# Step 0's normalisation, turn and query projection placed among the parts of batch 3 of the first layer, with value buffers exchanged and loads in batch 3

## The chip, the cores and the metric

The kernel runs on one core of one Trainium2 chip. The metric is the device time of one execution in microseconds (us), lower is better; "the time before" is the median of three executions.

The five engines run their own instruction lists in order and meet only through semaphores: TensorE (PE in the profile, with its weight loads as PEld), VectorE (DVE), ScalarE (ACT), GpSimd (POOL) and SyncE (SP), which here only issues DMAs. An instruction whose semaphore has not arrived holds up all that stands behind it in its engine's list.

## The reference

Four stages are added to a residual stream `x` of 4 batches, 512 tokens, width 128, each on the layer norm of the stream before it.

```python
x = x + _L0_xcond_ref(ctx, ln(x), cond, cond, ...)   # 16 heads of 64: queries from x, keys and values from ctx rows 512 + 77
x = x + _L0_ffn_ref(ln(x), ...)                       # ternary weights, activations rounded to 127 levels, relu squared
x = x + _L1_xcond_ref(ln(x), cond, ctx, masks, ...)   # 6 layers
x = x + _L1_ffn_ref(ln(x), ...)                       # 8 experts, each token goes to one

for i in range(6):                                    # inside _L1_xcond_ref, 16 heads of 8
    xn = _adaln(x, noise_emb, n1_w[i], n1_b[i])       # gain and bias of the norm come from emb @ w.T + b
    q, k, v = split(xn @ qkv_w[i].T); q, k = _rope(q), _rope(k)
    x = x + _attn(q, k, v, src_mask) @ so_w[i].T      # softmax over 512 keys
    xn = _adaln(x, ..., n2)                           # cross attention to 77 context rows, then
    x = x + _attn(_rope(xn @ cq_w.T), _rope(ctx @ ck_w.T), ctx @ cv_w.T, ctx_mask) @ co_w[i].T
    x = x + gelu(_adaln(x, ..., n3) @ f1_w[i].T + f1_b[i]) @ f2_w[i].T + f2_b[i]
```

## The kernel before

**Stages.** The first attention layer with its feed-forward part ("the first layer" here) is worked off batch by batch, `bt` = 0 to 3. For one batch there are 32 pairs of (head pair `u`, 128 queries `q`): `scores` (PE), `maximum` (DVE), `exp` (ACT), `divide` (DVE makes 1/sum, POOL multiplies), `turn` (PE transposes), `turned` (DVE and ACT copy), and 40 parts `weigh` (PE, weights times values), then four parts `out` (PE, L1402), the output projection. After the last `out` of batch 3, its feed-forward part `b_stats`, `b_norm`, `b_square`, `b_power`, `b_scale`, `b_quant`, `b_turn`, `b_up`, ... is still to come; it runs among the parts of the next stage.

The six later layers are 24 steps `m` = 4*layer + batch. A step's self attention is: `s_stats` (DVE) and `s_norm` (POOL, L2361 to L2367), `s_turn` (PE) and `s_mod` (ACT), the projections `qk` 0 and 1 (PE, L1614), the rotation `qk_rope` 0 to 3 (DVE, L2033), a swap of rows by four DMAs each for q and k (`q_swap`, `k_swap`, L1153), `q_thirds` and `k_thirds` (POOL, L2373 to L2383, a split of each float into three bf16 parts), six DMAs each that write the parts into the stacks `q_st` and `k_st` (`q_rows` L1197, `k_rows` L1208), then 64 parts `maximum` (PE L1467, DVE L1977), `shift` (POOL), `shift_turn` and `shift_out` (PE, ACT), one DMA `shift_rows` for each half (L1211), and 64 parts `scores` (PE L1455), `exp` (ACT L2197) and 16 `weigh` (PE L1487).

**Fixed rows.** Some rows of the stacks hold zeros, ones and the mask. `first_zeros` and `first_rows` write those of step 0. `other_rows` (18 DMAs of SP, L1104 to L1148) writes those of all other batches and of the cross attention; every `maximum` of a step above 0 waits for it (`zeroed`), and its DMAs stand in SP's one list like all the others.

**Gains.** `condition(i)` (PE, L1276) multiplies the norm weights `nT` with the condition vector in five pieces; ACT copies (L2111) and POOL adds the bias (L2325) as `gains`.

**What sets the order.** A table per engine gives each part a place and so an order in steady state. `PLACED_TENSOR`, `PLACED_SCALAR`, `PLACED_VECTOR`, `PLACED_POOL`, `PLACED_SYNC` override it around the seam between the stages: an entry `("maximum", 11, 0): [("b_turn", 0, None)]` says that `b_turn` 0 of the last batch runs just before `maximum` 11 of step 0. A PSUM bank is waited for by who writes it next (`free(b)`): `BANKS["qk"] = [0, 6]`, `BANKS0["out"] = [6]`, and `BANKS0["weigh"]` ends with bank 6.

**Value buffers.** The first layer's values lie in two buffers in turn. One of them is the space `wl` of the later layers' weights:

```python
handle.tensor_copy(v0[bt % 2][i][0:rows, 0:512], ...)   # batches 1 and 3 in wl
```

so that layer 0's weights of the next stage can be loaded only when batch 3's `weigh` is done (`av`).

Of the kernel before, what the change touches and what calls it, by code (L numbers as in the profile page):

```python
# [40 lines left out]
MAGIC = 1.5 * 2.0 ** 23  # L41
NORM_PIECES = ((0, 2), (2, 6), (6, 16), (16, 26), (26, 36))
# [54 lines left out]
def build(nc, a, out):  # L97

    ctx = ExitStack()
    with ctx:  # L100
# [5 lines left out]
        def bank(i):  # L106
            return psum[:, i, :]
# [55 lines left out]
        nT = A0[:, A_NT:A_NT + 6 * NL * D]  # L163
        early = (taken[0] - 4 * S - A_NT) // D
# [31 lines left out]
        lat_set, ctx_set, ffn_set = norm_set(), norm_set(), norm_set()  # L196
# [45 lines left out]
        st_s, mv_s, ve_s, rs_s = step_norm()  # L242
# [41 lines left out]
        DONE_ROWS = STEPS - B + 3  # L284

# [11 lines left out]
        def four(t):  # L297
# [219 lines left out]
            ("scores", 1, 0): [("maximum", 38, 0)],
            ("maximum", 40, 0): [("maximum", 39, 0)],
            ("maximum", 41, 0): [("scores", 2, 0)],
            ("scores", 3, 0): [("maximum", 42, 0)],  # L520
            ("weigh", 0, 0): [("scores", 7, 0), ("s_turn", 0, 1)],
            ("scores", 9, 0): [("maximum", 45, 0)],
            ("scores", 10, 0): [("maximum", 46, 0)],
            ("maximum", 47, 0): [("qk", 0, 1)],
            ("scores", 12, 0): [("maximum", 48, 0), ("scores", 11, 0)],
            ("scores", 13, 0): [("qk", 1, 1)],
            ("scores", 15, 0): [("weigh", 1, 0)],
            ("scores", 17, 0): [("scores", 16, 0)],
            ("scores", 19, 0): [("maximum", 50, 0)],
            ("maximum", 52, 0): [("maximum", 51, 0), ("weigh", 2, 0), ("v", 0, 1)],  # L530
# [18 lines left out]
            ("maximum", 17, 1): [("scores", 42, 0)],
            ("maximum", 20, 1): [("maximum", 19, 1), ("scores", 45, 0)],  # L550
            ("scores", 48, 0): [("maximum", 22, 1)],
            ("maximum", 24, 1): [("scores", 51, 0)],
            ("maximum", 26, 1): [("weigh", 11, 0)],
# [1989 lines left out]
```

## Time and profile before

| | |
|---|---|
| time before | 2364.84 us median (2360.6, 2364.84, 2368.64) |
| the profiled execution | 2367.46 us, of which its span (first to last instruction) 2365.3 us |
| busy share of the span | PE 94%, PEld 41%, DVE 82%, ACT 74%, POOL 46% |
| mean granted TensorE clock | 0.975 of full speed |
| busy tenths of PE in 40 slices of 59 us | 6999999999688999999999999999999999999979 |
| granted clock in the same slices | 9999999999589999999999999999999999999979 |
| the chain that ended last | PE 63%, DVE 14%, ACT 10%, DMA 4%, POOL 4%, issue 3% |

How to read it: each digit is a tenth of a slice, and a granted clock of 5 is the lower of TensorE's two levels. The slices 11 to 13 (591 to 768 us) are the seam between the first layer and step 0 to 2 of the next stage.

### The profile page before, as it was taken

The numbers are of one execution on the slowest core, as the hardware profiler recorded it, in microseconds if no ns is written. First come the engines' busy times: TensorE is split into PE (matmuls) and PEld (weight loads), VectorE is DVE, ScalarE is ACT, GpSimd is POOL, SyncE is SP. The second block draws the span as 40 slices with busy tenths as digits, with TensorE's granted clock in tenths as the row PEclk, the third lists the DMA queues.
The fourth block names the chain that finished last, engine by engine and source line by source line (L and its number), as shares of the span: only waits on it lengthen the run. The fifth ranks groups of instructions, "written<-read, shape, count | busy, mean of one in ns | idle before, by whom it ended". The sixth has DMA issues, their size and how long they took to land.

```text
span 2365.3 us, 46233 instructions
## 1 busy us (share of the span) xinstructions
PE 2218.9 (94%) x17034; PEld 960.1 (41%) x17034; DVE 1930.4 (82%) x3983; ACT 1761.9 (74%) x3601; POOL 1082.6 (46%) x1348
## 2 busy tenths in 40 slices
PE   6999999999688999999999999999999999999979
PEld 3455455545322333333343333333343334333336
DVE  6778889698778888888888888898888888888435
ACT  4778778696166778788888787887888887777744
POOL 3656556466334434434444443533454444432324
PEclk9999999999589999999999999999999999999979
DMA  2000000000312211212222321212222322111000
GB/s 84 2 1 1 1 2 1 30 1 20 90 50 63 82 50 54 65 46 72 62 67 69 82 63 48 67 51 66 54 74 63 81 63 66 49 49 52 25 23 19
DMA packets 108570, 113.07 MB, mean 48 GB/s; under 512 B 15809, under 2 KB 96951, under 8 KB 107319
## 3 DMA queue, kind: packets, MB, share of 16 engines
q1 hardware_dynamic: 108345, 110.12, 17.1%
q8 instruction: 135, 2.21, 0.4%
q14 instruction: 90, 0.74, 0.1%
HBM read 14.80 MB, written 1.05 MB: 7 GB/s over the span
## 4 chain that ended last, share of the span: by engine, by line
PE 63%; DVE 14%; ACT 10%; DMA 4%; POOL 4%; issue 3%; SPq 2%; DVEq 0%; POOLq 0%; ACTq 0%
PE psum L1487 11%; PE psum L1455 6%; PE psum L1467 6%; DVE A L1977 5%; PE psum L1258 4%; PE psum L1599 4%; PE psum L1591 4%; PE psum L1559 3%; PE psum L1388 3%; PE psum L1342 3%; DMA A<-A 3%; ACT A L2137 3%; DVE A L1999 3%; PE psum L1548 2%; PE psum L1354 2%
## 5 line engine op out<-in xcount | busy, mean ns | idle before, releaser
L1977 DVE TENSOR_REDUCE A<-psum 128x1 f32<-128x512 f32 x1536 | 969.9, 682 | 141.5 <-PE psum L1467 133.4
L2197 ACT ACTIVATE A<-psum 128x512 f32<-128x512 f32 x1536 | 821.4, 604 | 206.0 <-PE psum L1455 177.9
L1467 PE MATMUL psum<-A 64*128 64x512 bf16 x1536 | 421.8, 391 | 35.9 <-DVE A L1977 12.8
L1455 PE MATMUL psum<-A 64*128 64x512 bf16 x1536 | 403.9, 384 | 15.6 <-DVE A L1977 6.0
L1487 PE MATMUL psum<-A 128*9 128x512 f32 (+1 forms) x3072 | 405.2, 604 | 1.6 <-ACT A L2197 1.5
L2342 POOL TENSOR_TENSOR A<-A,rden 128x512 f32<-128x512 f32 x256 | 266.7, 1067 | 177.5 <-DVE rden L1862 176.7
L2373 POOL TENSOR_TENSOR A<-A 128x512 f32<-128x512 f32 (+1 forms) x78 | 96.6, 1239 | 301.8 <-DMA A<-A 291.8
L1467 PEld LDWEIGHTS psum<-A 64*128 64x128 bf16 x1536 | 105.1, 94 | 309.7 <-DVE A L1977 116.7
L2227 ACT ACTIVATE A<-psum 77x512 f32<-77x512 f32 x384 | 199.7, 598 | 30.3 <-PE psum L1548 29.7
L1455 PEld LDWEIGHTS psum<-A 64*128 64x128 bf16 x1536 | 103.5, 94 | 277.2 <-DVE A L1977 103.8
L2137 ACT ACTIVATE A<-psum,nm 128x512 f32<-128x512 f32 x256 | 176.0, 688 | 45.0 <-DVE nm L1850 44.1
L2386 POOL CAST A<-A 128x32 bf16<-128x32 f32 (+1 forms) x72 | 15.7, 218 | 384.3 <-DVE A L1999 197.9
L1999 DVE TENSOR_REDUCE A<-psum 128x8 f32<-128x616 f32 x192 | 149.9, 793 | 22.0 <-PE psum L1531 18.5
L1258 PE MATMUL psum<-ident,A 128*128 128x128 f32 x880 | 141.5, 288 | 21.0 <-DVE A L1724 14.5
L1846 DVE TENSOR_REDUCE mins<-psum 128x2 f32<-128x1024 f32 x128 | 155.2, 1212 | 5.4 <-PE psum L1342 5.2
L1342 PE MATMUL psum<-A 64*128 64x512 f32 x512 | 142.0, 617 | 1.8 <-DVE mins L1834 1.8
L1258 PEld LDWEIGHTS psum<-ident,A 128*128 128x128 f32 x880 | 96.1, 143 | 95.8 <-issue 55.4
L2361 POOL TENSOR_SCALAR A<-A 128x4 f32<-128x4 f32 x72 | 16.3, 227 | 213.0 <-DVE A L1967 213.0
L1548 PE MATMUL psum<-A 64*77 64x512 bf16 x384 | 104.6, 410 | 4.1 <-DMA A<-A 2.1
L1559 PE MATMUL psum<-A 77*32 77x512 f32 (+1 forms) x768 | 105.6, 623 | 1.7 <-ACT A L2227 1.6
L1354 PEld LDWEIGHTS psum<-ident,A 64*128 64x128 f32 x2048 | 76.0, 139 | 73.0 <-issue 48.9
L1591 PE MATMUL psum<-A,wl 128*128 128x512 f32 x192 | 97.0, 628 | 1.0 <-ACT A L2197 0.5
(209 smaller groups left out, 3743.4 us busy)
## 6 DMA issues: line engine op xcount, KB each, us to landing
A<-A SPq DMA_DIRECT2D x456, 128.0 KB, 2.4
A<-A SPq DMA_DIRECT2D x336, 64.0 KB, 2.0
A<-zero SPq DMA_DIRECT2D x51, 128.0 KB, 2.4
wl<-in_wl SPq DMA_DIRECT2D x6, 1024.0 KB, 5.8
A<-A SPq DMA_DIRECT2D x36, 78.0 KB, 2.1
A<-in_nT SPq DMA_DIRECT2D x1, 1664.0 KB, 6.8
A<-in_w SPq DMA_DIRECT2D x2, 512.0 KB, 7.0
A<-in_w SPq DMA_DIRECT2D x1, 1024.0 KB, 6.1
```

The costliest lines, as they stand in the source:

```text
L1258: t = handle.transpose(psum[:, b, q * P:(q + 1) * P], src[:, q, :], ident[:, :])
L1342: handle.matmul(bank(b), q_pair[lo:lo + HD0, u % 2, q * P:(q + 1) * P], k_pair[lo:lo + HD0, u % 2, 0:S], start=True, stop=True).then_inc(s ...
L1455: handle.matmul(bank(b), k_st[bt][lo:lo + ROW, h // 2, k * P:(k + 1) * P], q_st[m % 3][lo:lo + ROW, h // 2, :], start=True, stop=True).the ...
L1467: handle.matmul(bank(b), q_st[m % 3][lo:lo + ROW, pair, q * P:(q + 1) * P], k_st[bt][lo:lo + ROW, pair, :], start=True, stop=True).then_in ...
L1487: t = handle.matmul(psum[32 * j:32 * j + (HW if g % 2 else 32), b, :], values, pT[:, i % 2, j, :], start=k == 0, stop=k == QT - 1)
L1591: handle.matmul(bank(b), wcols(m, W_F1 + i * P, P), xnT_f, start=True, stop=True).then_inc(f1_ps, 1)
L1977: handle.tensor_reduce(nm[:, pair // 4, q, j, pair % 4:pair % 4 + 1], bank(BANKS["maximum"][i]), AX.X, ALU.max, negate=True).then_inc(mx, 1)
L1999: handle.tensor_reduce(cnm[:, :, :, i], both, AX.X, ALU.max, negate=True).then_inc(cm, 1)
L2137: handle.activation(p0[r][:, j, :], bank(BANKS0["scores"][i][j]), ACT.Exp, bias=nm0[:, r, j:j + 1], accum_out=c_p[:, n, j, q, C:CP]).then_ ...
L2197: handle.activation(pT[:, block % 2, i % GROUP, :], bank(BANKS["scores"][i]), ACT.Exp, scale=HD1 ** -0.5).then_inc(ex, 1)
L2227: handle.activation(cpT[0:C, g % 2, i % GROUP, :], psum[0:C, BANKS["cross_scores"][i], :], ACT.Exp, scale=HD1 ** -0.5).then_inc(cex, 1)
L2342: handle.tensor_tensor(p0[i % 4][:, j, :], p0[i % 4][:, j, :], rden[:, u % 2, j, q:q + 1].to_broadcast([P, S]), ALU.mult).then_inc(dp, 1)
```

## The change

All of it is at that seam.

1. Value buffers are exchanged: `v0[(bt + 1) % 2]`, so batches 0 and 2 use `wl` and batches 1 and 3 the other buffer.
2. Loads: when batch 2 is done, layer 0's weights go to `wl[:, 0]` and the first 16 pieces of `nT` to `wl[:, 1]`. The other 20 pieces and the small cross mask are loaded at the end of batch 3 (`late_loads`). The mask comes as 8 rows of 512 instead of 2 rows of 2048.
3. Step 0's `s_stats`, `s_norm`, `s_turn`, `s_mod`, `qk` 0 and `qk_rope` 0 and 1, `condition` and `gains` 0 and `fixed_rows` 0 run among the parts of batch 3. `qk` 1 stands between the last `weigh` and `out`.
4. The fixed rows of step 0 are written by separate parts `zero_q`, `rows_q`, `zero_k`, `rows_k`; `other_rows` is placed just before `q_swap` of step 1.
5. The orders of steps 0 to 4 are other tables.

```diff
-        v0[bt % 2]
+        v0[(bt + 1) % 2]
...
         PLACED_TENSOR = {
-            ("qk", 0, 0): [("condition", 0, None)],
-            ("v", 0, 0): [("condition", 1, None), ("condition", 2, None)],
-            ("maximum", 0, 0): [("condition", 3, None)],
-            ("maximum", 11, 0): [("b_turn", 0, None)],
+            ("turn", 16, -1): [("condition", 0, -1)],
+            ("weigh", 20, -1): [("s_turn", 0, 0)],
+            ("weigh", 31, -1): [("qk", 0, 0)],
+            ("out", 0, -1): [("qk", 1, 0)],
+            ("v", 0, 0): [("condition", 1, -1), ("condition", 2, -1)],
+            ("maximum", 0, 0): [("condition", 3, -1), ("condition", 4, -1)],
+            ("maximum", 16, 0): [("b_turn", 0, -1)],
...
         PLACED_VECTOR = {
+            ("divide", 14, -1): [("s_stats", 0, 0)],
+            ("divide", 26, -1): [("fixed_rows", 0, -1)],
+            ("divide", 30, -1): [("qk_rope", 0, 0)],
+            ("turned", 29, -1): [("qk_rope", 1, 0)],
...
         PLACED_POOL = {
+            ("divide", 39, -1): [("gains", 0, -1)],
+            ("divide", 40, -1): [("s_norm", 0, 0)],
+            ("shift", 0, 0): [("gains", 1, -1), ("b_power", 0, -1), ("gains", 2, -1), ("constants", 0, -1), ("b_power", 1, -1)],
...
         PLACED_SYNC = {
-            ("q_swap", 0, 0): [("first_rows", 0, 0)],
-            ("k_swap", 0, 0): [("q_zero", 0, 0)],
-            ("shift_rows", 0, 0): [("other_rows", 0, 0)],
+            ("q_swap", 0, 0): [("masks", 0, 0), ("weights", 0, 0), ("zero_q", 0, 0)],
+            ("k_swap", 0, 0): [("late_loads", 0, 0), ("rows_q", 0, 0)],
+            ("k_rows", 0, 0): [("zero_k", 0, 0), ("q_zero", 0, 0), ("rows_k", 0, 0)],
+            ("shift_rows", 0, 0): [("q_rows", 0, 0)],
+            ("q_swap", 0, 1): [("other_rows", 0, 0)],
...
+                if name == "late_loads":
+                    sp.wait_ge(av, B * NP0)
+                    sp.wait_ge(in_mask, 16)
+                    sp.wait_ge(in_late, 112)
+                    handle.dma_start(maskc_i[0:2, :], a["maskc"]).then_inc(in_mask, 16)
+                    handle.dma_start(norm_w(NORMS_FIRST, 6 * NL), a["nT"][:, NORMS_FIRST * D:]).then_inc(in_late, 16)
+                if name == "other_rows":
+                    sp.wait_ge(prep_ps, 1 + len(NORM_PIECES))
+                    sp.wait_ge(ow, B)
+                    sp.wait_ge(fixed, 3)
```

In the placements, the third number -1 stands for batch 3 of the first layer.

The order on TensorE at the end of batch 3, in the kernel before (L1388 is `weigh`, L1276 `condition`, L1402 `out`, L1258 `s_turn`, L1614 `qk`, L1622 `v`, L1467 `maximum`):

```order
L1388 MATMUL psum<-A 64x512 [waits tc_a]
L1388 MATMUL psum<-A 64x512
L1276 MATMUL psum<-condT,A 128x4 x2
L1402 MATMUL psum<-A 128x128 [waits av_a]
L1402 MATMUL psum<-A 128x128 x31
L1258 MATMUL psum<-ident,A 128x128 [waits s_y]
L1258 MATMUL psum<-ident,A 128x128 x3
L1276 MATMUL psum<-condT,A 128x4 [waits in_late]
L1276 MATMUL psum<-condT,A 128x4 x3
L1614 MATMUL psum<-A,wl 128x512 [waits in_wl,s_xn]
L1614 MATMUL psum<-A,wl 128x512 [waits x0]
```

The same place in the changed kernel, whose lines are 25 to 27 higher (L1411 is `weigh`, L1641 `qk` 1, L1423 `out`, L1301 `condition`, L1649 `v`, L1494 `maximum`):

```order
L1411 MATMUL psum<-A 64x512 [waits tc_a]
L1411 MATMUL psum<-A 64x512
L1641 MATMUL psum<-A,wl 128x512 [waits av_a]
L1423 MATMUL psum<-A 128x128 [waits qk_ro]
L1423 MATMUL psum<-A 128x128 x31
L1301 MATMUL psum<-condT,wl 128x4 x14
L1649 MATMUL psum<-wl,A 128x128 x4
L1301 MATMUL psum<-condT,A 128x4 [waits in_late]
L1301 MATMUL psum<-condT,A 128x4 x9
L1301 MATMUL psum<-condT,A 128x4 [waits g_copied]
L1301 MATMUL psum<-condT,A 128x4 x9
L1494 MATMUL psum<-A 128x512 [waits rows,k_rows,q_rows]
```

`qk` 1 has come ahead of `out`, and since both use bank 6, `out` now waits until DVE has read `qk` 1 (`qk_ro`); `s_turn` and `qk` 0 have gone up into batch 3.

SP's list between the rows of step 0 and the swaps of step 1, before (L1208 is `k_rows` of step 0, L1104 to L1148 `other_rows`, L1211 `shift_rows` 0 of step 0, L1153 `q_swap` of step 1):

```order
L1208 DMA A<-A 16x8x512 [waits sp_k]
L1104 DMA A<-zero 16x24x512 [waits prep_ps]
L1104 DMA A<-zero 16x24x512
L1104 DMA A<-zero 16x16x512
L1104 DMA A<-zero 16x32x284
L1104 DMA A<-zero 16x16x312
L1108 DMA A<-A 2x16x512 [waits zeroed]
...
L1148 DMA A<-A 2x16x312
L1211 DMA A<-A 16x4x512 [waits sh_T]
L1153 DMA A<-A 32x512 [waits qk_ro]
```

The same in the changed kernel (L1233 is `q_rows` of step 0, L1248 `shift_rows`, L1115 to L1181 `other_rows`, L1186 `q_swap` of step 1):

```order
L1233 DMA A<-A 16x8x512 [waits sp_q]
L1248 DMA A<-A 16x4x512 [waits sh_T]
L1115 DMA A<-zero 16x24x512 [waits fixed,ow,prep_ps]
L1115 DMA A<-zero 16x24x512
L1115 DMA A<-zero 16x16x512
L1115 DMA A<-zero 16x32x284
L1115 DMA A<-zero 16x16x312
L1119 DMA A<-A 2x16x512 [waits zeroed]
...
L1181 DMA A<-A 2x16x312
L1186 DMA A<-A 32x512 [waits qk_ro]
```

`shift_rows` 0 has moved ahead of the 18 DMAs of `other_rows`, which now stand between it and the swaps of step 1.

POOL's list from the split of step 0's q to its first shift, before (L2373 to L2383 are `q_thirds`, then `k_thirds`; L2311 is `b_power`; L2315 to L2317 `constants`; L2361 the start of `s_norm` of step 1):

```order
L2311 TENSOR_TENSOR A<-A,neg_half 128x4 [waits b_ve]
...
L2373 TENSOR_TENSOR A<-A 128x512 [waits q_swap,qk_ro]
...
L2311 TENSOR_TENSOR A<-A,neg_half 128x4 [waits b_ve]
L2373 TENSOR_TENSOR A<-A 128x512 [waits k_swap,qk_ro]
...
L2315 MEMSET A 128x256 [waits ow]
L2316 MEMSET A 128x1344
L2317 MEMSET A 128x2016
L2361 TENSOR_SCALAR A<-A 128x4 [waits s_mv,s_yT]
```

The same in the changed kernel (L2394 to L2404 are the splits, L2332 is `b_power`, L2336 to L2338 `constants`, L2407 `shift`):

```order
L2394 TENSOR_TENSOR A<-A 128x512 [waits q_swap,qk_ro]
...
L2394 TENSOR_TENSOR A<-A 128x512 [waits k_swap,qk_ro]
...
L2332 TENSOR_TENSOR A<-A,neg_half 128x4 [waits b_ve]
...
L2336 MEMSET A 128x256 [waits ow]
L2337 MEMSET A 128x1344
L2338 MEMSET A 128x2016
L2332 TENSOR_TENSOR A<-A,neg_half 128x4 [waits b_ve]
L2407 CAST A<-A 128x8x4 [waits mx]
```

Both `b_power` now stand behind both splits, and `constants` has come in between the two of them.

## Rows read from the trace of the kernel before

**Rows 1.** Windows: length, busy PE, PEld, DVE, ACT, POOL, clock, DMA share, GB/s

```profile
540.00:580.00 40.00, 39.36 (x375) 19.58 (x372) 32.23 (x66) 32.75 (x94) 28.61 (x28) 1.00 0.01 2
...
680.00:694.00 14.00, 10.96 (x52) 4.45 (x52) 9.19 (x15) 6.28 (x10) 3.62 (x6) 0.63 0.06 17
```

**Rows 2.** Timeline, end of batch 3: start, length, engine; in brackets its wait

```profile
584.47 1.03 PE L1388 MATMUL psum<-A 77*64 77x512 f32 x4
585.55 0.60 ACT L2158 ACTIVATE A<-psum 128x512 f32<-128x512 f32 x1 [2.89 <-PE psum L1388]
586.20 7.41 PE L1402 MATMUL psum<-A 128*128 128x128 f32 x64 [0.16 <-ACT A L2158]
593.65 0.69 DVE L1874 TENSOR_TENSOR x_res<-x_res,psum 128x512 f32<-128x512 f32 x1 [1.83 <-PE psum L1402]
```

**Rows 3.** Timeline, step 0's q and k up to its first maximum

```profile
598.84 0.69 DVE L2033 TENSOR_TENSOR A<-psum,sinT 128x512 f32<-128x512 f32 x1 [2.98 <-PE psum L1614]
603.99 1.27 POOL L2373 TENSOR_TENSOR A<-A 128x512 f32<-128x512 f32 x1 [0.24 <-DMA A<-A]
612.03 4.04 SPq L1208 DMA_DIRECT2D A<-A  x6
617.94 1.03 PE L1467 MATMUL psum<-A 64*128 64x512 bf16 x4 [6.24 <-issue]
```

**Rows 4.** Timeline, feed-forward part of batch 3 up to DVE's first maximum

```profile
602.57 0.86 DVE L1706 BATCH_NORM_STATS2 A<-A 128x6 f32<-128x128 f32 x4
605.31 0.17 DVE L1736 TENSOR_SCALAR A<-A 128x4 f32<-128x4 f32 x1
609.05 1.04 POOL L2311 TENSOR_TENSOR A<-A,neg_half 128x4 f32<-128x4 f32 x1
610.12 1.28 ACT L2162 ACTIVATE A<-A 128x128 f32<-128x128 f32 x4 [7.06 <-POOL A L2311]
611.43 1.12 DVE L1886 TENSOR_TENSOR A<-A 128x512 f32<-128x512 f32 x1 [5.95 <-ACT A L2162]
614.42 4.69 DVE L1945 TENSOR_SCALAR A<-A,small 128x128 f32<-128x128 f32 x4
621.15 18.22 DVE L1977 TENSOR_REDUCE A<-psum 128x1 f32<-128x512 f32 x30
```

**Rows 5.** One line of DVE, all 32 instances: shortest, median, longest in ns

```profile
L1945 DVE TENSOR_SCALAR A<-A,small x32: 269/479/4241, 204.9 to 678.5; 128x128 f32<-128x128 f32 x16, 128x512 f32<-128x512 f32 x16
```

**Rows 6.** Timeline, POOL's divides late in batch 3

```profile
542.31 4.18 POOL L2342 TENSOR_TENSOR A<-A,rden 128x512 f32<-128x512 f32 x4 [4.04 <-DVE rden L1862]
...
572.91 6.16 POOL L2342 TENSOR_TENSOR A<-A,rden 128x512 f32<-128x512 f32 x6 [2.13 <-DVE rden L1862]
```

**Rows 7.** Timeline of SP's DMA issues, then what SP waited for, 615 to 665

```profile
616.12 7.88 SPq L1104 DMA_DIRECT2D A<-zero  x5
...
630.13 5.95 SPq L1120 DMA_DIRECT2D A<-A  x3
...
638.31 1.32 SPq L1148 DMA_DIRECT2D A<-A  x1
645.84 0.61 SPq L1211 DMA_DIRECT2D A<-A  x1
660.06 2.50 SPq L1153 DMA_DIRECT2D A<-A  x4
...
SPq L1153 <- DVE A L2033: 14.2, 1, 14.2
...
SPq L1108 <- DMA A<-zero: 3.9, 1, 3.9
```

**Rows 8.** Timeline, step 1's q and k up to its first maximum

```profile
656.69 1.10 PE L1614 MATMUL psum<-A,wl 128*128 128x512 f32 x2 [0.35 <-ACT A L2197]
...
665.96 1.26 POOL L2373 TENSOR_TENSOR A<-A 128x512 f32<-128x512 f32 x1
...
678.83 0.60 PE L1467 MATMUL psum<-A 64*128 64x512 bf16 x3
```

More of the change, by code:

```diff
@@ L516, in build @@
+            ("maximum", 29, 0): [("b_up", 3, -1)],
             ("maximum", 37, 0): [("maximum", 36, 0)],
[L517 to L518 removed]
+            ("maximum", 38, 0): [("scores", 0, 0)],
             ("maximum", 41, 0): [("scores", 2, 0)],
             ("scores", 3, 0): [("maximum", 42, 0)],
[L521 removed]
+            ("scores", 6, 0): [("maximum", 43, 0), ("maximum", 44, 0)],
@@ L522, in build @@
+            ("scores", 8, 0): [("s_turn", 0, 1)],
             ("scores", 9, 0): [("maximum", 45, 0)],
[L523 to L530, printed above, removed]
+            ("maximum", 47, 0): [("qk", 0, 1), ("maximum", 46, 0)],
@@ L548, in build @@
             ("weigh", 8, 0): [("maximum", 15, 1)],
[L549 to L553, printed above, removed]
+            ("weigh", 9, 0): [("maximum", 17, 1)],
+            ("o_turn", 0, 0): [("maximum", 18, 1)],
+            ("maximum", 20, 1): [("maximum", 19, 1)],
@@ L850, in build @@
         PLACED_VECTOR = {
-            ("qk_rope", 0, 0): [("fixed_rows", 0, None), ("x_out", 0, None), ("b_stats", 0, None)],
-            ("qk_rope", 2, 0): [("b_norm", 0, None)],
-            ("max", 0, 0): [("b_square", 0, None), ("b_quant", 0, None), ("s_stats", 0, 1)],
-            ("max", 30, 0): [("b_affine", 0, None)],
-            ("max", 33, 0): [("b_stats2", 0, None)],
-            ("max", 35, 0): [("b_stats2", 1, None)],
-            ("max", 36, 0): [("b_stats2", 2, None)],
-            ("max", 40, 0): [("b_stats2", 3, None)],
@@ new lines, in build @@
+            ("divide", 26, -1): [("fixed_rows", 0, -1)],
+            ("divide", 30, -1): [("qk_rope", 0, 0)],
+            ("turned", 29, -1): [("qk_rope", 1, 0)],
+            ("max", 0, 0): [("x_out", 0, -1), ("b_stats", 0, -1), ("b_norm", 0, -1), ("b_square", 0, -1), ("s_stats", 0, 1),
+                ("fixed_rows", 1, -1), ("b_quant", 0, -1)],
+            ("max", 30, 0): [("b_affine", 0, -1)],
+            ("max", 31, 0): [("b_stats2", 0, -1)],
+            ("max", 35, 0): [("b_stats2", 1, -1)],
@@ L1189, in part @@
                         sp.wait_ge(sh_rows, 32 * (m - 2))
+                    if m == 0:
+                        for done in (pq, pk, pc):
+                            sp.wait_ge(done, NP0 * B)
+                    else:
+                        sp.wait_ge(ow, B)
+                        sp.wait_ge(fixed, 2)
                     sp.wait_ge(q_rows, 112 * m)
@@ L1449, in part @@
                 l, bt = divmod(m, B)
+                if name == "warm":
+                    b = EXPERTS_BANKS["warm"][m // (STEPS - 1)][i]
+                    free(b)
+                    for _ in range(4):
+                        handle.matmul(bank(b), zero16[:, 0:P], zero16[:, :], start=True, stop=True)
+                    owner.pop(b, None)
                 if name == "scores":
```

490 lines of the change are left out of this document (247 added, 243 removed).

## The prediction

> **What bounds the kernel now.** I read the page's slices first: TensorE is busy nine tenths nearly everywhere except at both ends and in the three slices from 591 to 768 us, where its granted clock falls too. So a change at this seam can only be worth what the seam wastes. The windows come next: late in batch 3 PE is busy 39.4 of 40 us, so work put there is not free on PE, while POOL has 11 idle us in the same stretch [rows 1]. The timeline then gives two chains that run side by side from the last `weigh` to the first maximum of step 0.
>
> Chain one is step 0's q and k. The last `weigh` ends at 585.5, `out` runs from 586.2 to 593.6 [rows 2]; only then come `s_turn` and `qk`, the rotation at 598.84, the split on POOL at 603.99, the last six row DMAs at 612.03, and PE's first maximum at 617.94, after 6 us in which it did nothing [rows 3]. Chain two is the feed-forward part of batch 3: `x_out` at 593.65 [rows 2], `b_square` ready at 605.5, but `b_power` 1 only at 609.05, as it stood behind the split of q; `b_scale` at 610.12; `b_quant` from 611.43; DVE's first maximum at 621.15 [rows 4]. Chain two ends later, by 2.6 us of maxima that already lay ready. It decides.
>
> Behind both comes a third list that no engine waits for yet: SP's. `other_rows` took it from 616.12 to 639.6, 23.5 us, with 3.9 us of waiting for its own zeros. After that SP waited for DVE 14.2 us, until 660.06 when step 1's first rotation was done [rows 7]. The reader is to see that this slack of SP is as large as all that the change can win.
>
> **The change part by part.**
>
> *Batch 3 gets longer.* PE takes up `condition` 0, `s_turn` and `qk` 0. A projection like `qk` takes 1.1 us where it stands at step 1 [rows 8]; the other two are smaller. Bounds 0 (all inside PE's waits) and 3.3; I take 2.1, near the top, because PE is full. `condition` 0 stood between `weigh` and `out`, so there it gives back what it costs here, which I count below. POOL's `s_norm` and `gains` 0 are some 4 us and are put exactly where POOL waited 4.04 us for DVE; before POOL becomes the one waited for, at 572.91, it still has waits, the last of 2.13 [rows 6]. Cost nothing; without that cover 4. DVE's additions (`s_stats`, two rotations at 0.69 [rows 3], `fixed_rows` 0) are some 4 us in a stretch where DVE is idle 7.8 of 40 us [rows 1]; I count them within the 2.1.
>
> *`out` waits.* Before, `out` began when ACT had copied the last `weigh` [rows 2]. Now `qk` 1 needs that same copy (bank 6), and `out` needs bank 6 back from DVE: 1.0 for `qk` 1 and 1.3 for two rotations, 2.3 us. `out` ends at 593.6 + 2.1 + 2.3 = 598.0.
>
> *Chain one* now runs beside `out`: ACT's copy is done at 588.2, k's rotation starts at 589.2, its split on POOL 5.15 later as before (603.99 - 598.84 [rows 3]), at 594.4, and it ends near 599.9. SP then has k's six row DMAs and behind them q's six, 4.0 each; with the fixed rows ahead of them they start near 598 and the first maximum could run at 598 + 8.1 + 1.9 = 608.
>
> *Chain two* decides again. From the end of `out`: `x_out` and `b_stats` 2.2, `b_power` 0 1.0 after 0.3 of waiting for POOL's split of k, `b_norm` 1.4, `b_square` 2.9 (602.57 to 605.48 [rows 4]; POOL's `constants` fall into it and are over before it), `b_power` 1 1.0, `b_scale` 1.3. `b_quant` and what follows took 8.5 us until `s_stats` of step 1 began, of which 4.69 for four small operations [rows 4]; one of them took 4.24 where the shortest of the line takes 0.27 [rows 5], and POOL was filling memory then. That filling now lies earlier, and `s_stats` 1 is ahead of `b_quant`: 4.5. With four hand-overs of 0.2 this is 15.4, so DVE's first maximum comes at 613.4 instead of 621.15, **7.7 us earlier**.
>
> *What is late next.* Step 0's maxima and `b_up` keep their distances, so `shift_rows` 0, 24.7 us behind the first maximum before (645.84 [rows 7]), is issued at 613.4 + 24.7 + 0.5 (one more statistics operation ahead of the 32nd maximum) = 638.6; 0.6 later SP starts `other_rows`. It has stood idle for some 30 us by then, but its list had the shift first. 639.2 + 23.5 = 662.7: only now do the swaps of step 1 go out, though DVE has had the rotation since 660.06 - 7.7 = 652.4. Before they went out at 660.06. Then POOL: four swaps take 2.5, landing 1.6, so its split starts at 666.8; before it started at 665.96, held by work of its own [rows 8]. PE's first maximum of step 1 came 12.9 us later, at 678.83 [rows 8]; now at 679.7. Behind it in PE's list stand the rest of step 0's scores and `weigh`, the second shift's transposes and `b_turn2`, so ACT and DVE run dry too, DVE after its 64 maxima, near 671. PE stands some 8 us. **The 7.7 us are given back, and 0.9 more.**
>
> One correction: of the three mask DMAs (5.95 us, L1120 [rows 7]) none should need more than the 0.7 that the DMAs beside them take, so up to 3.9 may not come again. I take half of it, 1.9.
>
> The Trainium skill weighs the other way: "DMA: Bandwidth & Descriptors", section "Issuing engines are not separate DMA queues", says that the sequencer's time to start a DMA is usually small beside the DMA itself. By that rule the 18 DMAs would cost next to nothing in SP's list and the kernel would win all of the 7.7 us, 2357; the issue rows, 23.5 us for the block, say otherwise for this kernel.
>
> **The sum.** +0.9 - 1.9 = -1.0 us: the profiled execution's span of 2365.3 becomes 2364.3, its time of 2367.5 becomes 2366.5. That execution lies 2.6 above the median of the runs, so the median becomes 2363.8. What remains of the pipeline is the same work in nearly the same order; I give it nothing.
>
> **The rivals.**
>
> *The gain comes through* (faster). If `other_rows` holds SP for less than 13 us (639.2 to 652.4), the swaps of step 1 follow DVE and all 7.7 us stay: 2357, and up to 9.8 with batch 3's additions hidden: 2355. For it: 3.9 of the 23.5 us are a wait and 3.9 are two odd issues, leaving 15.7. Against: the five zero DMAs alone took 7.9 us to issue and 3.9 more to land, with no stack row in between.
>
> *A new wait takes the old one's place* (slower). If chain two does not shorten, because `b_power` 0 and 1, now behind the split of k and behind `constants`, come as late as 609, the first maximum stays at 621. Then SP's block starts at 647 and step 1's maxima come 8.6 us later: 2373. It decides from a first maximum later than 620. Against it: 6 us of margin in the sum.
>
> *The clock* (slower by less). PE standing still for 8 us falls to its lower level; from 680 to 694 it already worked at 0.63 with 11.0 of 14 us busy [rows 1]. If the lower level lasts through all of the next 20 us, with PE the bound, this costs some 5 us: 2369, and with batch 3's additions at 3.3 and more, just over 2371.
>
> **How the numbers follow.** A measurement of this kernel can tell about 0.3%, 7 us, from no change. Forecast (step 1's rows decide, the gain given back, including a partial gain below 7 us): 0.57. Gain through: 0.28. New wait: 0.08. Clock with its additions, past 7 us: 0.07. So faster 0.28, same 0.57, slower 0.15. The likeliest case's own range is 2359 to 2368. The range must reach to most of the faster case (2355) and to the clock case, 2371.
>
> **What would show it.** DVE's first maximum near 613, `out` starting 2 to 3 us after ACT's last copy; SP's `shift_rows` near 639 and right behind it the block, ending near 660; the first maximum of step 1 between 676 and 681 with PE, DVE and ACT idle for 5 to 9 us before it. The forecast is wrong if SP's block is done before DVE's rotation of step 1, or if the first maximum of step 0 is not earlier than 618.

## The result, and the profile after

The changed kernel is slower: 2373.93 us median of 4 runs (2373.11 to 2377.41), beside 2363.09 for the kernel before on the same chip; the ratio is 1.0044, 95% interval 1.003 to 1.0057. A second measurement gave 2374.33 beside 2363.58, ratio 1.0043 (1.0028 to 1.0059). That is 10.8 us where 1 us less was forecast, and 3 us past the end of the range.

First the page of the changed kernel: span, busy times, busy tenths of PE, granted clock, and the shares of the chain that ended last.

```profile
span 2371.8 us, 46239 instructions
...
PE 2211.7 (93%) x17034; PEld 957.5 (40%) x17034; DVE 1928.1 (81%) x3983; ACT 1762.7 (74%) x3601; POOL 1083.4 (46%) x1348
...
PE   6999999999778999999999999999999999999979
...
PEclk9999999999689999999999999999999999999989
...
PE 58%; DVE 15%; ACT 9%; POOL 7%; DMA 5%; SPq 3%; issue 3%; DVEq 0%; POOLq 0%; ACTq 0%
```

The reader is to see two things. Between the start and the end of the execution the seam is still the one weak place. And in the chain that ended last, PE has given up 5 points of its 63 to POOL (7 for 4), DMA (5 for 4), DVE, and SPq, the issuing of DMAs (3 for 2): more of the end is decided by waits for copies and transfers.

The timeline of TensorE in batch 3 and up to step 0's first maximum (start, length, instruction; in brackets its wait) answers to [rows 2, 3]; L1284 is `s_turn`, L1411 `weigh`, L1641 `qk`, L1423 `out`, L1301 `condition`, L1494 `maximum`.

```profile
547.39 1.01 PE L1284 MATMUL psum<-ident,A 128*128 128x128 f32 x4 [3.14 <-DVE A L1953]
548.34 4.05 PE L1411 MATMUL psum<-A 128*64 128x512 f32 x12
...
588.64 4.51 PE L1411 MATMUL psum<-A 128*64 128x512 f32 x20
593.85 1.13 PE L1641 MATMUL psum<-A,wl 128*128 128x512 f32 x2 [0.70 <-ACT A L2184]
596.36 7.41 PE L1423 MATMUL psum<-A 128*128 128x128 f32 x64 [1.38 <-DVE A L2064]
...
614.58 4.43 PE L1301 MATMUL psum<-condT,A 128*128 128x4 f32 x20 [3.88 <-ACT gb L2137]
618.94 1.04 PE L1494 MATMUL psum<-A 64*128 64x512 bf16 x4
```

The last `weigh` ends at 588.64 + 4.51 = 593.15, 7.6 later than before. `out` waits for `qk` 1 as forecast. From the last `weigh` to DVE's first maximum, at 619.58, it is 26.4 us, where before it was 35.6 [rows 2, 4]. So the chain did become 9.2 shorter, but batch 3 used up 7.6 of that ahead of it, and 1.6 are left (619.58 for 621.15).

Next, the same two places of the timeline that [rows 7, 8] show before: SP's list between `shift_rows` 0 (L1248) and the rows of step 1, and PE's first maximum of step 1 (L1494). L1115 are zeros, L1119 ones, L1126 masks, L1181 the small cross mask, L1186 the swaps of q and k. As the counts in this view show, `other_rows` is 15 DMAs, five of zeros and ten of rows. The 18 that stands above and in the expectations is what the semaphore `zeroed` counts to, and three zero DMAs of step 0 are in that; for the same reason the 13 row DMAs are 10.

```profile
644.17 0.53 SPq L1248 DMA_DIRECT2D A<-A  x1
644.82 7.50 SPq L1115 DMA_DIRECT2D A<-zero  x5
656.61 2.16 SPq L1119 DMA_DIRECT2D A<-A  x3
658.81 6.77 SPq L1126 DMA_DIRECT2D A<-A  x3
665.62 2.07 SPq L1119 DMA_DIRECT2D A<-A  x3
667.73 0.55 SPq L1181 DMA_DIRECT2D A<-A  x1
668.32 6.17 SPq L1186 DMA_DIRECT2D A<-A  x8
...
686.64 0.58 PE L1494 MATMUL psum<-A 64*128 64x512 bf16 x1 [8.80 <-DMA A<-A]
```

The block takes 668.32 - 644.82 = 23.5 us, as before; 4.3 of them SP waits for the zeros to land. The swaps of step 1 go out 8.3 us later than they did, eight at once, so q and k are both late, and PE stands still for 8.80 us. The chain of waits from 643 to 690 (start, length, what) runs straight through SP:

```profile
by line: SPq L1126 14.2%; DMA A<-zero 12.8%; SPq L1115 11.9%; DMA A<-A 9.1%; SPq L1119 8.6%; SPq L1186 5.4%; POOL A L2394 5.3%; POOL A L2400 5.1%; POOL A L2404 5.0%; issue 4.5%; PE psum L1514 3.8%; POOL A L2398 3.2%; PE psum L1656 2.8%; POO
...
650.57 6.02 DMA A<-zero
656.61 0.58 SPq L1119
...
658.81 3.78 SPq L1126
662.62 2.00 SPq L1126
...
664.67 0.91 SPq L1126
...
673.52 1.27 POOL A L2394
```

### The profile page after: what moved, and what is told of

Its sections match the earlier page's. It is cut to its first block, busy times and chain, and to the rows that moved or that the text cites. A ratio compares the mean times of both kernels' runs of the same rounds, so it can differ in the third digit from the quotient of the medians.

```text
span 2371.8 us, 46239 instructions
## 1 busy us (share of the span) xinstructions
PE 2211.7 (93%) x17034; PEld 957.5 (40%) x17034; DVE 1928.1 (81%) x3983; ACT 1762.7 (74%) x3601; POOL 1083.4 (46%) x1348
## 3 DMA queue, kind: packets, MB, share of 16 engines
q1 hardware_dynamic: 108357, 110.12, 17.1%
## 4 chain that ended last, share of the span: by engine, by line
PE 58%; DVE 15%; ACT 9%; POOL 7%; DMA 5%; SPq 3%; issue 3%; DVEq 0%; POOLq 0%; ACTq 0%
PE psum L1514 10%; DVE A L2005 5%; PE psum L1482 5%; PE psum L1494 5%; DMA A<-A 4%; PE psum L1284 4%; PE psum L1626 4%; PE psum L1411 4%; PE psum L1618 4%; PE psum L1367 3%; PE psum L1586 3%; DVE A L2027 3%; ACT A L2163 2%; PE psum L1379 2%; POOL A L2394 2%
## 5 line engine op out<-in xcount | busy, mean ns | idle before, releaser
L1494 PE MATMUL psum<-A 64*128 64x512 bf16 x1536 | 420.3, 390 | 43.3 <-DMA A<-A 17.1
L2394 POOL TENSOR_TENSOR A<-A 128x512 f32<-128x512 f32 (+1 forms) x78 | 96.8, 1242 | 318.6 <-DMA A<-A 318.6
L1494 PEld LDWEIGHTS psum<-A 64*128 64x128 bf16 x1536 | 104.5, 94 | 317.4 <-DVE A L2005 116.8
L2407 POOL CAST A<-A 128x32 bf16<-128x32 f32 (+1 forms) x72 | 15.8, 220 | 393.0 <-DVE A L2027 197.9
L1284 PE MATMUL psum<-ident,A 128*128 128x128 f32 x880 | 140.6, 287 | 25.6 <-DVE A L1746 14.7
L1284 PEld LDWEIGHTS psum<-ident,A 128*128 128x128 f32 x880 | 95.2, 142 | 101.3 <-issue 57.6
L2382 POOL TENSOR_SCALAR A<-A 128x4 f32<-128x4 f32 x72 | 16.5, 229 | 208.4 <-DVE A L1995 208.2
L1895 DVE COPY A<-psum 128x512 f32<-128x512 f32 x128 | 85.4, 684 | 21.5 <-PE psum L1379 20.6
```

Source lines behind the costliest of these rows:

```text
L1284: t = handle.transpose(psum[:, b, q * P:(q + 1) * P], src[:, q, :], ident[:, :])
L1494: handle.matmul(bank(b), q_st[m % 3][lo:lo + ROW, pair, q * P:(q + 1) * P], k_st[bt][lo:lo + ROW, pair, :], start=True, stop=True).then_in ...
```

## The experiments

The theory after this reading has two parts. (1) `s_turn` stands where its PSUM bank isn't free, which makes batch 3 longer by its wait and by the lower clock behind it. (2) `other_rows` behind `shift_rows` 0 holds the swaps of step 1. The rivals: batch 3 is longer just by the work that PE took up; or the zero and row DMAs slow down what runs beside them wherever they stand.

### One part undone at a time

`turn_later` moves one part on PE, behind the `weigh` that it stood ahead of:

```diff
-            ("weigh", 20, -1): [("s_turn", 0, 0)],
+            ("turn", 20, -1): [("s_turn", 0, 0)],
```

> The changed kernel with step 0's s_turn placed behind weigh 22 of batch 3 instead of ahead of weigh 20. Theory: s_turn stood 3.14 us on PE because its PSUM bank (7) is that of b_down of batch 2, which DVE had not read yet; the three weigh behind it then ran at the lower clock (4.05 us instead of 2.79). Both go: the last weigh ends 4.4 us earlier (588.8), everything behind it too, step 0's first maximum near 615.2, SP's block near 640, time 2369.5 (-4.4 against the changed kernel). Rival, the wait is covered by work elsewhere (batch 3 is longer because of PE's added work alone): last weigh at 592 or later, 2373.

2368.86 us, ratio to the kernel before 1.0013 (1.0 to 1.0025). Its timeline of PE:

```profile
544.15 2.79 PE L1411 MATMUL psum<-A 128*64 128x512 f32 x12
547.35 0.63 PE L1284 MATMUL psum<-ident,A 128*128 128x128 f32 x4 [0.41 <-DVE A L1953]
...
682.80 0.58 PE L1494 MATMUL psum<-A 64*128 64x512 bf16 x1 [9.93 <-DMA A<-A]
```

The same 12 `weigh` matmuls start 4.2 earlier and take 2.79 instead of 4.05, step 0's first maximum is at 615.10 on PE instead of 618.94, and the stall at step 1 stays. The first part of the theory holds, and its rival (last `weigh` at 592 or later) falls. Of the 4.4 us expected at the end of batch 3, 3.4 came (`qk` 1 at 590.48 for 593.85): `s_turn` still waits 0.41, and the part behind it 0.95 for ACT.

`block_early` moves one part on SP:

```diff
-            ("shift_rows", 0, 0): [("q_rows", 0, 0)],
-            ("q_swap", 0, 1): [("other_rows", 0, 0)],
+            ("shift_rows", 0, 0): [("q_rows", 0, 0), ("other_rows", 0, 0)],
```

> The changed kernel with other_rows (18 DMAs) ahead of shift_rows 0 of step 0 in SP's list. Theory: SP issues the block from 612.5 to 636, the swaps of step 1 follow DVE's rotation near 659, PE's wait of 8.80 us at 677.8 shrinks to under 1 and step 1's first maximum comes at 677 to 679 instead of 686.6: 2365 (-8 to -9.5). Rival, the DMAs of the block slow down the row DMAs or the engines beside them as much: first maximum of step 1 past 684, 2372 or more.

2365.59 us, ratio 0.9999 (0.9986 to 1.0011). SP's issues, and behind them PE (in this kernel the lines are one lower: L1493 is `maximum`, L1247 `shift_rows`, L1185 the swaps):

```profile
618.83 7.46 SPq L1114 DMA_DIRECT2D A<-zero  x5
630.50 2.15 SPq L1118 DMA_DIRECT2D A<-A  x3
632.69 6.79 SPq L1125 DMA_DIRECT2D A<-A  x3
...
641.63 0.55 SPq L1180 DMA_DIRECT2D A<-A  x1
643.95 0.61 SPq L1247 DMA_DIRECT2D A<-A  x1
658.34 5.37 SPq L1185 DMA_DIRECT2D A<-A  x8
...
677.48 0.38 PE L1493 MATMUL psum<-A 64*128 64x512 bf16 x1
```

The block runs as long as before, but beside maxima that need nothing of SP; `shift_rows` 0 isn't later, the swaps follow DVE's rotation, and step 1's first maximum comes at 677.48 instead of 686.64 with no wait. The block begins at 618.83 and not at 612.5 as expected, since it waits for the last `condition`, and it fits ahead of the shift with 1.8 us to spare.

`both` has the two edits together.

> Both edits, s_turn behind weigh 22 and other_rows ahead of shift_rows 0. Theory: the two add up, -12.5 against the changed kernel, 2361, which is 2 below the kernel before (ratio 0.999). Rival, one bound hides the other (step 1 held by DVE or POOL in both): 2364 to 2366.

2361.21 us, ratio 0.9981 (0.9969 to 0.9993). By the ratios to the kernel before, the first edit is worth 0.31% and the second 0.45%, and the two together 0.63%: they add up as far as these intervals can tell, and give a kernel that is faster than the one before by 0.2%.

That is what the medians say. The trace of `both` itself doesn't show the first gain: `qk` 1 starts at 592.08 and PE's first maximum at 617.93, only 1.0 earlier than in the changed kernel, and step 1's first maximum is at 676.72. TensorE was at its lower clock twice in it where `turn_later` was not, behind waits of 0.41 and 0.95 us at 549.6 and in `out`, which took 8.97 us instead of 7.41. So moving `s_turn` takes away the bank's wait in every trace, and the lower clock behind it in most: from 543 to 560 us the granted clock was 1.00 in five of the six traces with this edit and 0.90 in the one of `both`, and 0.80 or 0.90 in all six without it.

### How long must the block be to hurt

Three kernels start from the changed kernel, without the edits above, and shorten what stands behind `shift_rows` 0. `zeros_early` leaves the ten row DMAs behind it:

```diff
-            ("shift_rows", 0, 0): [("q_rows", 0, 0)],
-            ("q_swap", 0, 1): [("other_rows", 0, 0)],
+            ("shift_rows", 0, 0): [("q_rows", 0, 0), ("other_rows", 0, 0)],
+            ("q_swap", 0, 1): [("other_ones", 0, 0)],
...
                     zeros(A_CK, A_V, SHIFT_SLOT, B * CP, zeroed)
+                if name == "other_ones":
                     sp.wait_ge(zeroed, 8 * 16)
```

> The changed kernel with the 5 zero DMAs of other_rows ahead of shift_rows 0 and the 13 row DMAs where they were, behind it. What stands behind the shift takes 11.7 us (656.61 to 668.28 in the changed kernel): 644.8 + 11.7 = 656.5, before DVE's rotation of step 1 (659.06). Theory: swaps of step 1 at 14.4 us behind the shift as with the whole block early, first maximum 33.5 behind it, 2365.6. Rival, the row DMAs themselves slow what runs beside them: over 35 behind it, 2368 or more.

2367.1 us, ratio 1.0006 (0.9991 to 1.002). Its first maximum of step 1 is at 677.48, 33.4 us behind the shift. `part_late` leaves three zero DMAs and six of ones behind the shift, and moves two zero DMAs and the four of masks ahead of it:

```diff
-            ("shift_rows", 0, 0): [("q_rows", 0, 0)],
+            ("shift_rows", 0, 0): [("q_rows", 0, 0), ("mask_part", 0, 0)],
...
+                if name == "mask_part":
+                    zeros(A_K + A_STACK, A_CQ, MASK_SLOT, S, zeroed)
+                    zeros(A_CQ, A_V, MASK_SLOT, 284, zeroed)
+                    sp.wait_ge(zeroed, 5 * 16)
...
```

> The changed kernel with other_rows cut in two: 2 zero DMAs, the 3 mask DMAs and the small cross mask ahead of shift_rows 0, the other 12 (3 zero DMAs, then 9 of ones) behind it, ahead of q_swap of step 1. The theory of SP's time says: what stands behind the shift takes 3 * 1.5 + up to 3.9 of waiting + 9 * 0.65 = 14 us, 644.8 + 14 = 659, just when DVE's rotation of step 1 is ready (659.06), so PE's wait of 8.80 us goes as when the whole block is early: first maximum of step 1 at 678 to 680, 2366. Rival, it isn't the length of what stands there but that any of these DMAs (their landing, or `zeroed`) comes after the shift: first maximum past 683, 2370 or more.

2365.93 us, ratio 1.0006 (0.9989 to 1.0023). I had counted 14 us behind the shift and it was 16.5: the six ones that now follow each other took 9.30 instead of 2.2 and 2.1 for three each. So PE waited 1.94 us. The first row shows its three mask DMAs, here with no ones ahead of them:

```profile
627.98 1.71 SPq L1126 DMA_DIRECT2D A<-A  x3
...
646.77 0.59 SPq L1250 DMA_DIRECT2D A<-A  x1
647.40 3.15 SPq L1115 DMA_DIRECT2D A<-zero  x3
654.51 9.30 SPq L1119 DMA_DIRECT2D A<-A  x6
663.86 6.85 SPq L1188 DMA_DIRECT2D A<-A  x8
...
682.54 0.37 PE L1496 MATMUL psum<-A 64*128 64x512 bf16 x1 [1.94 <-DMA A<-A]
```

`small_ones` keeps all 15 DMAs in their place and makes six of the row DMAs write one head pair instead of 24, 16 or 8. It leaves out the ones and masks of all other head pairs, so what it computes differs from the reference:

```diff
-                    ones(A_Q + A_STACK, A_K, slice(MASK_SLOT, P, ROW), S, zeroed)
+                    ones_few(A_Q + A_STACK, A_K, slice(MASK_SLOT, P, ROW), S, zeroed)
...
-                        mask_rows(b, zeroed)
+                        handle.dma_start(few(k_st[b][MASK_SLOT:P:ROW, :, :]), mask_b[2 * b:2 * b + 2, :].unsqueeze(1)).then_inc(zeroed, 16)
```

> The changed kernel, with the first 6 of the 13 row DMAs of other_rows (3 of ones, 3 of the mask) writing one head pair each instead of 24, 16 or 8; the rest of these rows keeps zeros, so the later layers' logits are others than the reference's. The number of DMAs and their places stay. Question: what holds SP for 3.78 and 2.4 us at the fourth and fifth of them. Theory A, the transfers: rows on two or three partitions move at some 25 GB/s with a tenth of the DMA time busy, and SP can't issue further until they have drained; then the six take 6 * 0.55 = 3.3 us instead of 8.9, the block 18, the swaps go out near 662.7 and the first maximum of step 1 comes 5.6 earlier, near 681: 2368.5. Theory B, a price per mask DMA: the three mask DMAs still take near 6.8 us, 2374.

2368.31 us, ratio 1.0019 (1.0002 to 1.0035). The same number of DMAs, with less in them (L1134 the ones, L1184 the masks, which took 2.16 and 6.77 in the changed kernel). Theory A holds, with 2368.31 for the 2368.5 expected:

```profile
646.14 7.48 SPq L1115 DMA_DIRECT2D A<-zero  x5
657.90 2.05 SPq L1134 DMA_DIRECT2D A<-A  x3
660.00 1.59 SPq L1184 DMA_DIRECT2D A<-A  x3
661.63 2.15 SPq L1119 DMA_DIRECT2D A<-A  x3
...
664.41 6.51 SPq L1194 DMA_DIRECT2D A<-A  x8
...
682.79 0.58 PE L1502 MATMUL psum<-A 64*128 64x512 bf16 x1 [3.55 <-DMA A<-A]
```

All five kernels in one table, times counted from the issue of `shift_rows` 0:

| | SP's list behind the shift takes | swaps of step 1 | first maximum of step 1 |
|---|---|---|---|
| `block_early` | 0 | +14.4 | +33.5 |
| `zeros_early` | 11.5 | +14.3 | +33.4 |
| `part_late` | 16.5 | +17.1 | +35.8 |
| `small_ones` | 18.3 | +18.9 | +37.3 |
| changed kernel | 23.5 | +24.2 | +42.5 |

Up to some 14 us nothing happens; beyond that nearly every microsecond on SP is one on PE. The order of the lists is what costs, and its price is what stands behind the shift less 14. That also falsifies the rival of contention: in `block_early` the whole block runs, with its full length, beside step 0's maxima, and in `zeros_early` the ten row DMAs stand at the same place of the list as in the changed kernel (12 us earlier in time), and nothing is late in either. The reverse test, the block put behind the shift in the kernel before, was written, and 2372.5 expected of it, but there is no time for it: in that kernel the source of the mask rows lies in memory that `exp` of step 0 overwrites, so the move alone makes a race. (The changed kernel holds the masks elsewhere.) So the price of the block is shown by taking it out of the changed kernel, not by adding it to the one before.

### What is left at the seam

Three kernels start from `both`. `both_bank` gives `out` of batch 3 a bank of its own:

```diff
-                    b = BANKS0["out"][0]
+                    b = 1 if bt == B - 1 else BANKS0["out"][0]
```

> Both edits (s_turn behind weigh 22, other_rows early), and `out` of batch 3 in bank 1 instead of 6, so that it no longer waits for DVE's read of qk 1 (1.38 us). Theory: out ends 1.4 earlier, but b_power 0 stands behind POOL's split of k, which hangs on qk 1 and not on out, and DVE waits for it anyway (1.15 us in the run with both edits): first maximum of step 0 earlier by at most 0.4, 2361. Rival, out is the head of the chain that decides: 1.4 earlier, 2359.8.

2361.03 us, ratio 0.9985 (0.9974 to 0.9995), no change against `both`. The wait of `out` is gone, but from `qk` 1 to the first maximum PE takes 613.82 - 589.19 = 24.6 us, as in `turn_later` (615.10 - 590.48). DVE's wait for `b_power` 0 grew from 1.49 (`turn_later`) to 2.77 instead. So `out` isn't the head of the chain that decides now; the head is `qk` 1, through k's rotation, its swap and POOL's split, behind which `b_power` 0 stands.

`both_gains` lets ACT copy `condition` 3 ahead of `b_scale`:

```diff
-            ("shift_out", 0, 0): [("b_scale", 0, -1), ("gains", 3, -1), ...
+            ("shift_out", 0, 0): [("gains", 3, -1), ("b_scale", 0, -1), ...
```

> Both edits, and on ACT gains 3 ahead of b_scale of batch 3 instead of behind it, so that condition 4 (4.43 us on PE, ahead of step 0's first maximum) doesn't wait 2.54 us for a copy that stands behind b_power 1. Theory: PE's first maximum 1.6 to 2.3 earlier, and DVE, ready 1.12 us before it, gains just these 1.1: 2360. Rival, DVE's maxima catch up within step 0 (DVE waits there for ACT and the first layer's up-projection anyway): no change, 2361.

2360.53 us, ratio 0.9982 (0.9971 to 0.9992). In its timeline `condition` 4 waits 0.61 us instead of 2.54 in `both`:

```profile
608.14 4.43 PE L1300 MATMUL psum<-condT,A 128*128 128x4 f32 x20 [0.61 <-ACT gb L2136]
612.50 1.04 PE L1493 MATMUL psum<-A 64*128 64x512 bf16 x4
```

From `qk` 1 to PE's first maximum it is 23.3 us instead of 24.6, and DVE's first maximum, which no longer waits for PE, comes 24.6 us behind `qk` 1 instead of 25.3 (613.72 - 589.16, and 615.74 - 590.48 in `turn_later`). That is 0.7 of the 1.1 us expected; the medians can't show it, and don't tell the theory from its rival.

`all_three` has the bank, the copy and `b_power` 0 ahead of `gains` 1 on POOL.

> Both edits, out in bank 1, gains 3 ahead of b_scale, and on POOL b_power 0 ahead of gains 1. Theory: 1.1 from the copy and 0.5 from POOL (b_power 0 no longer behind two small additions; out early enough for it): 1.6 less than with both edits alone, 2359.6. Rival, none of these waits decides: 2361 to 2362.

2360.3 us, ratio 0.998 (0.9968 to 0.9991). Against `both_gains` nothing is won: from `qk` 1 to the first maximum it is 23.9 us. `b_power` 0 now starts 12.6 us behind `qk` 1 instead of 13.1, but two of DVE's small groups behind it (L1757 and L1989) took 1.87 and 1.80 us where they took 0.81 and 0.86 in `both_gains`. They ended as POOL's filling of memory did (608.13), beside which the slow operation of [rows 4, 5] ran too. The four kernels lie between 2360.3 and 2361.2 and can't be told apart.

### The levels once more

> The changed kernel once more, unedited, on the chip of the next run, for a level beside it: the two edits of `both` were worth 12 us by the sum of their waits (8.8 less 0.6, and 3.14 + 1.26). If so, this stands 8 to 11 us above the kernel before (ratio 1.0035 to 1.0047) and 10 to 13 above the next run. Rival, the first measure of the changed kernel (1.0044) was high by chance: ratio under 1.003.

The changed kernel: 2374.33 us, ratio 1.0043 (1.0028 to 1.0059). The rival (under 1.003) falls, though the interval just reaches it.

> The kernel of both_gains once more (s_turn behind weigh 22, other_rows early, gains 3 ahead of b_scale). Theory: step 0's first maximum is 8 earlier than in the kernel before, and step 1's 4 to 5 earlier: ratio to the kernel before 0.998, about 2360.5, and 10 to 13 us below the changed kernel on the same chip. Rival, the gain before was within the spread: ratio 0.9995 or more.

The kernel of `both_gains`: 2358.67 us beside 2363.58, ratio 0.9983 (0.9967 to 0.9999), and 15.7 below the changed kernel on the same chip, more than the 10 to 13 expected.

> The kernel before once more, unedited, for a second trace of it. In the traces so far the changed kernel is 5.8 us behind the kernel before when steps 1 to 5 end and 12.6 behind when step 18 ends, and every kernel built from the changed one loses 4 to 7 us in the same stretch against the one trace of before. Theory A, that trace is a quick one there: this one ends step 18 some 3 to 5 us later than 2083.5, with steps 0 to 5 within 1. Theory B, the changed tables or timing cost a few us in the steady steps: it ends step 18 within 1.5 of 2083.5.

Its 2365.46 us beside 2363.22 (ratio 1.0015, 0.9992 to 1.0038) is the same kernel twice. Its trace ends step 18 at 2024.0, against 2023.6 in the first, and is within 1.3 us of it at the ends of steps 0 to 18. So the first trace of before isn't a quick one, and theory A falls. The ratio of 1.0015 for one kernel against itself also says how far to trust a single ratio: a gain of 0.2% isn't shown by one of them, but by the five from 0.9980 to 0.9985 together. (The expectation named 2083.5 for the end of step 18; that is the end of step 19.)

## Why the prediction was wrong

*What bounds the kernel*, right. SP's list was named as the third chain and it became the one that decides; the gain of the seam was given back there, as the forecast said. `block_early` shows this part by itself: step 1's first maximum 9.2 us earlier, and a ratio lower by 0.45%.

*Batch 3 gets longer*, **the step that failed**. The prediction gave it 2.1 us, bounds 0 and 3.3, as the PE time of `condition` 0, `s_turn` and `qk` 0. It was 7.65:

| | us |
|---|---|
| the trace starts batch 3 later | 0.3 |
| `condition` 0 and `s_stats` (PE waits 0.56 for DVE) | 1.0 |
| `s_turn` waits for its bank | 3.14 |
| `s_turn` itself, mostly at the lower clock (0.63 in `turn_later`) | 1.0 |
| 12 matmuls of `weigh` at the lower clock, 4.05 for 2.79 | 1.26 |
| `qk` 0 and the rest | 0.95 |

The term took in only the work, and not the bank that the work is written to. `s_turn` and `b_down` of batch 2 use the same bank, 7, and PE's next write of it waits for `b_out` on DVE (L1953). `b_down` was done at 541.8, but DVE read it at 546.57, behind the reductions of batch 3's maxima. Before, the twelve `weigh` stood there and needed no such bank. The upper bound was as wrong as the value, since it took the added parts' own length for the worst case. `turn_later`, which moves `s_turn` behind those twelve `weigh`, shows that this was the larger part: `qk` 1 comes 3.4 us earlier. In the 9 us around that wait the granted clock was 0.81 of full speed, and 1.00 in `turn_later` (windows of the two kernels, 543 to 552; columns as in [rows 1]):

```profile
543.00:552.00 9.00, 5.86 (x21) 2.06 (x18) 5.32 (x13) 6.34 (x19) 6.57 (x7) 0.81 0.01 3
```

```profile
543.00:552.00 9.00, 7.64 (x69) 3.77 (x66) 6.83 (x16) 7.46 (x23) 7.21 (x8) 1.00 0.01 3
```

*`out` waits 2.3*, right: 2.5. It ended at 603.8 instead of 598.0, nearly all of it by batch 3. But the chain that this fed was taken for the deciding one, and `both_bank` shows that it isn't.

*Chain two*, right in size: 15.4 from the end of `out` to DVE's first maximum was forecast, 15.8 measured, 1.1 of it a wait for PE's `condition` 4 that wasn't in the sum. The rest was 0.7 shorter than forecast, so that the totals agree is in part luck. The small operation that had taken 4.24 us [rows 5] took no more than 1.37 now, and the four together 0.88 in place of 4.69 [rows 4].

*What is late next*, right in kind, with one term too small. The block took the 23.5 us forecast. From the swaps to the first maximum I took 17.0 and it was 18.3: eight swaps now follow each other on SP where before four went out alone, so POOL's split started 5.2 us behind them instead of 4.1.

*The correction*, wrong: half of the 3.9 us of two long mask issues was taken off, as not coming again. They came again, 3.78 and 2.00 us here. The three masks took 6.0 us in both traces of before and 6.6 to 6.8 in every later trace in which three full DMAs of ones are issued just ahead of them. Without these the three masks, with their full rows, took 1.71 us (`part_late`).

The sum with what was measured: -1.0, and 5.5 for batch 3, 0.2 for `out`, 0.4 on chain two, -0.5 up to the shift, 1.3 behind the swaps, 1.9 for the correction, is +7.8: just how much later step 1's first maximum is (686.64 for 678.83). The medians' 10.8 us hold more than that. POOL's last addition of a step (x24; first and last start) tells how far a kernel is:

```profile
L2417 POOL TENSOR_TENSOR x_st<-x_st,f2b x24: 1261/1270/1281, 826.7 to 2312.2; 128x512 f32<-128x512 f32 x24
```

```profile
L2438 POOL TENSOR_TENSOR x_st<-x_st,f2b x24: 1262/1272/1282, 831.2 to 2318.7; 128x512 f32<-128x512 f32 x24
```

(The first row is the kernel before, the second the changed one.) At the end of step 0 the changed kernel is 4.4 behind, at the ends of steps 1 to 5 5.6 to 6.1, of step 10 10.1, of step 18 12.6; its second trace gives 6.0, 6.7 to 8.2, 8.8 and 13.9. At the very end the granted clock differs from trace to trace (0.86 to 0.93 from 2200 to 2350 us in these four), so that a single span says little. So of the 7.8 us at step 1's first maximum some 6 are left when steps 1 to 5 end, and some 6 more are lost by step 18, though both kernels run the same lists from step 6 on. Part of it is chance: step 10 took 70.9 us at a clock of 0.98 in the changed kernel and 69.0 at 1.00 in the kernel before, whose second trace has 70.9 at 0.98 too. Another part is waits of PE for a DMA, in step 17 (0.20 us in the kernel before, the first row, and 1.87 in the changed one) and in step 18, where before there was none (third row):

```profile
1881.82 0.32 PE L1531 MATMUL psum<-A 64*128 64x77 bf16 x8 [0.20 <-DMA A<-A]
```

```profile
1893.46 0.32 PE L1558 MATMUL psum<-A 64*128 64x77 bf16 x8 [1.87 <-DMA A<-A]
...
2006.30 0.37 PE L1494 MATMUL psum<-A 64*128 64x512 bf16 x1 [0.88 <-DMA A<-A]
```

The first differs from trace to trace (up to 2.07 us). The second isn't chance: it is 0.87 to 1.64 us in all twelve traces of the changed kernel and the kernels made from it, and in neither of before, and step 18 takes 77.5 to 79.7 us in the twelve and 76.5 in the two. Why these DMAs land later stays open, and so does the rest of what the steady steps lost. The prediction gave this term nothing ("the same work in nearly the same order"), and that failed too: the medians hold 10.8 - 7.8 = 3.0 us of it.

The prediction's own sign of failure came: step 0's first maximum was not earlier than 618. Of the rivals, *a new wait takes the old one's place* ended nearest (2373), and a first maximum at 619.58 is close to its 621. But its mechanism isn't what decided: `b_power` 1 did start only at 612.09, right behind `constants`, but DVE's `b_square`, which it needs, ended only at 611.99. What delayed both was mostly ahead of them, as `out` ended 5.8 later than forecast. So that its number fits is in the main luck. *The clock* (2369, and just over 2371 with the additions of batch 3 at their upper bound) pointed at batch 3 rightly, but its own part didn't come: PE did stand for 8.80 us, but in the 20 us from step 1's first maximum on the granted clock was 0.89, and 0.74 in the same 20 us before. *The gain comes through* asked for less than 13 us on SP; the table puts the limit at some 14, and the block took 23.5. The rule of the Trainium skill that was weighed ("DMA: Bandwidth & Descriptors", "Issuing engines are not separate DMA queues") would have given 2357; the block's 23.5 us on SP came as the rows said. But the rule is nearer to the truth than the prediction put it: 4.3 of the 23.5 us are a wait for zeros to land, and 5.2 more go when six DMAs carry less (`small_ones`).

## What to carry to other kernels

When a part moves, look up the buffer or bank that it writes, who last used it, and when that user's reader is done; the length of the part's own work is no upper bound of what it costs. When a wait goes, take the lists of the queues that have been slack and count from the last thing that holds them to the next thing that somebody waits for; if that is longer than the new slack, move the long part ahead of the holder before making the change. A long stretch of DMA issues belongs where its engine waits for nothing else.

## What the runs showed of the hardware

An issue on SP isn't of constant length; it hangs on what the DMAs just ahead of it carry. Three mask DMAs of 16 KB took 3.78, 2.00 and 0.91 us behind three DMAs of ones. The same three with the same 16 KB took 1.71 in all where no ones were ahead of them (`part_late`), and 1.59 where ones and masks both carried one head pair each (`small_ones`). The zeros show it too: in the changed kernel the first two took 0.56 and 0.62 us to issue, the next two 1.84 and 2.56 (the chain of waits from 643 to 690), and two by themselves 1.22 in all (`part_late`, at 621.65). While the rows of the changed kernel were under way the DMA engines were a tenth busy and moved some 24 GB/s, beside 150 for the zeros, which go to 16 partitions (the DMA view of the changed kernel, 656 to 668: busy tenths and GB/s in 40 slices):

```profile
DMA  2000001011111111111111111311111010101111
GB/s 44 0 0 0 0 0 31 20 27 27 20 24 24 20 24 24 20 24 24 20 24 24 20 20 24 79 24 24 24 24 24 21 27 20 48 14 20 17 31 59
```

The Trainium skill ("DMA: Bandwidth & Descriptors", "Why a DMA increments its semaphore by 16 and not by 1") says that a DMA is spread over the largest number of engines up to 16 that divides the outermost dimension of both its sides, so a transfer of two partitions would use two. The tenth of the engines' time agrees with it; that SP is held because these few engines are behind is my reading, shown only in so far as less data ahead took the hold away.

And the lower level (1.2 GHz) followed a wait of 3.14 us in an otherwise full TensorE: the 12 matmuls behind it took 4.05 us instead of 2.79. In the trace of `both` it followed waits of 0.41 and 0.95 us at the same place (four matmuls of 77 columns took 2.09 us instead of 1.35), and in `turn_later`, with the same two waits, it didn't.
